# Twelve-sublayer decoder: in two mixture-of-experts sublayers, the late chunks' reciprocal standard deviation moves from GpSimd's power to VectorE and ScalarE's root

## The reference, cut to what matters

```python
def _layernorm(x, axis=-1, eps=1e-05):
    m = jnp.mean(x, axis=axis, keepdims=True)
    v = jnp.var(x, axis=axis, keepdims=True)
    return (x - m) / jnp.sqrt(v + eps)
...
x = _layernorm(x + _L1_ffn_ref(x, ...), axis=-1)     # sublayer 6
...
x = _layernorm(x + _L3_ffn_ref(x, ...), axis=-1)     # sublayer 12, the last
```

```python
def _L1_ffn_ref(x, router_w, router_b, weights1, bias1, weights2, bias2):   # 32 experts, hidden 32
    logits = x_flat @ router_w.T + router_b
    routed_idx = jnp.argmax(logits, axis=-1)
    h = jax.nn.relu(x_flat @ w1 + b1); y = jax.nn.relu(h @ w2 + b2)         # for each expert
    out_flat = y_all[routed_idx, jnp.arange(n)]

def _L3_ffn_ref(x, wg, W1, b1, W2, b2):                                     # 8 experts, hidden 512
    scores = jax.nn.softmax(xf @ wg, axis=-1); top1 = jnp.argmax(scores, axis=-1)
    h = jax.nn.gelu(jnp.einsum('ecd,edf->ecf', eb, W1) + b1[:, None, :], approximate=False)
    y = jnp.einsum('ecf,efd->ecd', h, W2) + b2[:, None, :]
    out_flat = jnp.where(valid[:, None], gathered, 0.0) * combine_w[:, None]
```

## Time and profile before

| | us |
|---|---|
| median of 3 runs | 3607.47 |
| lowest and highest of them | 3604.95, 3610.28 |
| profiled execution, its own time | 3619.05 |
| span of its trace | 3616.9 |
| granted TensorE clock, mean | 0.885 of full speed |
| sublayer 6: first late gather to the last copy's end | 1823.14 to 1881.59 |
| last sublayer: last tile's eviction to the last normalisation's end | 3564.43 to 3607.76 |

### The profile page before, as it was taken

How to read it: one execution, slowest core, us unless ns; L and a number is a source line. 1 busy time by engine, 2 the same in 40 slices (tenths; PEclk the granted TensorE clock), 3 DMA queues, 4 the chain that set the end, 5 groups by cost and what they waited for, 6 DMA issues and landing times. The chain is left out here.

```text
span 3616.9 us, 83245 instructions
## 1 busy us (share of the span) xinstructions
PE 2818.4 (78%) x28638; PEld 1992.1 (55%) x28638; DVE 2157.7 (60%) x5986; ACT 1818.0 (50%) x3448; POOL 1838.9 (51%) x1774
## 2 busy tenths in 40 slices
PE   2259985698999799953529998997888779992993
PEld 2258974475666466632416665654444446662893
DVE  2101324655888688862337886777999778872124
ACT  0024543553666566611216665775567776660451
POOL 3721245544888755525465555664133755555226
PEclk9679998898999899975559999998999899995997
DMA  8246763120111111114611112221000012212584
GB/s 296 86 135 217 233 199 90 39 8 14 43 47 46 55 51 70 67 40 136 164 53 43 56 54 68 89 87 44 1 1 1 8 30 73 76 54 88 178 249 128
DMA packets 321561, 308.86 MB, mean 85 GB/s; under 512 B 110950, under 2 KB 244489, under 8 KB 320908
## 3 DMA queue, kind: packets, MB, share of 16 engines
q1 hardware_dynamic: 279644, 255.42, 22.9%
q0 software_dynamic: 16384, 33.59, 3.1%
q10 hardware_dynamic: 25264, 16.40, 1.5%
HBM read 167.28 MB, written 60.69 MB: 63 GB/s over the span
## 5 line engine op out<-in xcount | busy, mean ns | idle before, releaser
L956 DVE TENSOR_TENSOR moe_first_tile_y<-moe_first_out_ps,moe_first_expert_w 128x256 f32<-128x256 f32 x85 | 35.7, 423 | 377.7 <-PE moe_first_out_ps L1092 248.1
L1092 PE MATMUL moe_first_out_ps<-moe_first_expert_w,moe_first_hid 128*128 128x128 f32 x1360 | 181.7, 280 | 75.0 <-issue 73.5
L1092 PEld LDWEIGHTS moe_first_out_ps<-moe_first_expert_w,moe_first_hid 128*128 128x128 f32 x1360 | 174.2, 196 | 85.8 <-issue 80.2
L814 POOL DMA_INDIRECT moe_first_token_y<-slot_y,moe_first_slots x128 | 124.6, 974 | 175.0 <-DMA slot_y<-moe_first_tile_y 137.0
L1913 POOL TENSOR_TENSOR causal_k_blocks<-causal_k_T,headmask 128x1024 f32<-128x1024 f32 x64 | 121.5, 1899 | 96.5 <-PE causal_scores L1518 94.5
L1165 POOL DMA_INDIRECT slot_x<-x_tok,moe_first_slots x128 | 123.5, 965 | 87.7 <-DVE moe_first_slots L928 49.3
L1913 POOL TENSOR_TENSOR alibi_k_blocks<-alibi_k_T,headmask 128x1024 f32<-128x1024 f32 x64 | 121.3, 1898 | 91.3 <-PE alibi_scores L1518 90.0
L1913 POOL TENSOR_TENSOR full_k_blocks<-full_k_T,headmask 128x1024 f32<-128x1024 f32 x64 | 120.8, 1898 | 82.2 <-PE full_scores L1518 80.0
L3211 PE MATMUL L_ffn_experts<-weights_odd,x_T 128*128 128x512 f32 x256 | 138.1, 622 | 11.6 <-ACT L_ffn_expert_out L3311 11.5
L1913 POOL TENSOR_TENSOR keys_k_blocks<-keys_k_T,headmask 128x1024 f32<-128x1024 f32 x64 | 120.9, 1900 | 46.7 <-PE keys_scores L1518 45.6
L3134 DVE SCALAR_TENSOR_TENSOR L_ffn_combined<-L_ffn_expert_out,L_ffn_mix,L_ffn_combined 128x128 f32<-128x128 f32 x448 | 139.0, 373 | 3.9
(11 more groups left out here) (634 smaller groups left out, 9005.9 us busy)
## 6 DMA issues: line engine op xcount, KB each, us to landing
moe_first_expert_w<-in_L_attn_experts SPq DMA_DIRECT2D x85, 578.0 KB
moe_last_expert_w<-in_L_ffn_experts SPq DMA_DIRECT2D x53, 578.0 KB
moe_first_tile_x<-slot_x SPq DMA_DIRECT2D x85, 128.0 KB
slot_y<-moe_first_tile_y SPq DMA_DIRECT2D x85, 128.0 KB
slot_x<-blank ACTq DMA_DIRECT2D x2, 4992.0 KB
L_ffn_tile_x<-slot_x SPq DMA_DIRECT2D x32, 256.0 KB
slot_y<-L_ffn_tile_y SPq DMA_DIRECT2D x32, 256.0 KB
moe_last_tile_x<-slot_x SPq DMA_DIRECT2D x53, 128.0 KB
```

The lines of the kernel that those rows point to most:

```text
L814: pool.indirect_dma_start(y_in[:, p, k, r, :], None, slot_y[part][0:NTS[part] * SLOT_TILE, :], bass.IndirectOffsetOnAxis(slots[:, part, r, ...
L956: dve.tensor_tensor(y_out[:, q, :, :], out_bank[j % 2][:, 0:SLOT_TILE].rearrange("p (s d) -> p s d", s=SPAN), over(wall[:, j % RING, 2 * F ...
L1092: last = pe.matmul(out_bank[j % 2][:, D * s:D * s + D], hid[:, j % 3, b, TILE * s:TILE * s + TILE], wall[:, j % RING, FF + D * b:FF + D * ...
```

## The change

For the late chunks of the two sublayers, `inverse_std` on GpSimd is dropped. `own_std` on VectorE adds epsilon, waits for ScalarE's root (`std_act`) and takes the reciprocal; VectorE then normalises the same chunk at once, ahead of the next chunk's sum. GpSimd's late loop holds gathers alone. ScalarE in sublayer 6 runs the root of chunk c + 1 ahead of the copy of chunk c. Early chunks, and `moe_first`, stay as they were.

```diff
@@ class RowTail
+        if n_early is not None:
+            self.n_early, self.std, self.std_done = n_early, sb("ln_std", [128, 2, PER]), sem("ln_std_done")
...
+    def own_std(self, dve, c):
+        p = c % 2
+        dve.wait_ge(self.moments_done, c + 1)
+        dve.tensor_scalar(self.ve[:, p, :], self.mv[:, p, :, 1], LN_EPS, None, ALU.add).then_inc(self.ve_done, 1)
+        dve.wait_ge(self.std_done, c + 1 - self.n_early)
+        dve.reciprocal(self.rstd[:, p, :], self.std[:, p, :]).then_inc(self.rstd_done, 1)
+
+    def std_act(self, act, c):
+        p = c % 2
+        act.wait_ge(self.ve_done, c + 1)
+        act.activation(self.std[:, p, :], self.ve[:, p, :], ACT.Sqrt).then_inc(self.std_done, 1)
@@ moe, VectorE
                 for c in late:
                     combine(dve, c)
-                    if c != late[0]:
-                        tail.normalise(dve, c - 1)
-                if late:
-                    tail.normalise(dve, late[-1])
+                    tail.own_std(dve, c)
+                    tail.normalise(dve, c)
@@ moe, ScalarE
                 for c in late:
+                    tail.std_act(act, c)
                     tail.copy_transposed(act, c, route_bank)
@@ moe, GpSimd
-                for c in late:
-                    if c + 1 < CHUNKS:
-                        gather(pool, c + 1, range(PER))
-                    tail.inverse_std(pool, c)
+                for c in late[:-1]:
+                    gather(pool, c + 1, range(PER))
@@ moe_small, ScalarE
+                tail.std_act(act, late[0])
                 for c in late:
+                    if c != late[-1]:
+                        tail.std_act(act, c + 1)
                     tail.copy_transposed(act, c, xT_bank)
@@ moe_small, GpSimd
                     if (c + 1) % PC:
                         gather(c + 1)
-                    tail.inverse_std(pool, c)
+                    if c not in late:
+                        tail.inverse_std(pool, c)
```

More of the change, by code:

```diff
@@ L573, with __init__ @@
 class RowTail:
-    def __init__(self, sub, final, on_act=False):
+    def __init__(self, sub, final, on_act=False, n_early=None):
         self.net, self.final, self.on_act = sub.net, final, on_act
@@ L724, in moe @@
         y_in = sub.sb("token_y", [128, 2, PER, top, D])
-        tail = RowTail(sub, final)
+        tail = RowTail(sub, final, n_early=None if hand_over else 0)
         sub.ctx = ctx
@@ L784, in moe @@
         held = range(FIRST, CHUNKS)
+        if not hand_over:
+            tail.n_early = FIRST
         after_tile = {due(c): c for c in range(FIRST)}
@@ L2673, in moe_small @@
         y_in = sb("token_y", [128, 2, PER, D])
-        tail = RowTail(sub, final)
+        tail = RowTail(sub, final, n_early=PC)
         out_banks = ctx.enter_context(nc.psum_tensor(f"{name}_out_ps", [128, 4, 512], F32))
```

## The result

| | before | after |
|---|---|---|
| median, us | 3606.21 (4 runs, 3602.99 to 3610.28) | 3582.34 (4 runs, 3579.23 to 3584.26) |
| ratio | | 0.9936, 95% interval 0.9922 to 0.9949 |
| span of the profiled execution | 3616.9 | 3577.2 |
| sublayer 6, first late gather to the next sublayer's first operation | 1823.14 to 1887.19, 64.05 | 1805.20 to 1858.50, 53.30 |
| last sublayer, chunk 10's first gather to the end | 3563.53 to 3616.9, 53.4 | 3533.88 to 3577.2, 43.3 |

The change saves 23.9 in the medians, 18 to 28 by the interval. A second timing of the same kernel, in a later series on a chip on which the kernel before had a median of 3619.07, gave 3600.10, a ratio of 0.9952 (0.9936 to 0.9967), 19.0 less.

What follows compares the result with a forecast made beforehand. GpSimd's issue of gathers was taken to set the pace in both stretches. Layer 1's 9.3 and the last sublayer's 8.0 gave 17.2 (rounded terms) off the median 3607.47: 3590.3, bounds 3588.3 to 3595, with scatter 3585.5 to 3598.

Steps and rivals of the forecast that it cites:

- gathers of sublayer 6: Layer 1's late gathers on GpSimd, without powers between them, end 8.2 us earlier (6.6 to 9.7).
- root's way: Both ends, chunk 15's moments to normalisation: 1.48 becomes 0.70 via VectorE and ScalarE, 0.78 less each.
- gathers of the last sublayer: Last sublayer's late gathers on GpSimd, without powers between them, end 7.2 us earlier (5.9 to 7.4).
- End of layer 1: TensorE's last transposes: chunk 14's earlier copy frees the bank before the last normalisation ends, some 0.3 more saved.
- hits: Gathers starting just behind VectorE's sum take 1.47, costing 0.52 each; none to six in layer 1, three taken, 1.56.
- Hidden, with 0.7 us to spare: VectorE waiting out the root: last-sublayer chunk takes 4.3 against 5.02 of the gathers, so no cost.
- the 26 scatters: Last sublayer's row scatter, 26 seen in one go, later ones still 0.96 + 0.30: no sign of long goes slowing.
- signs of being wrong: Profile after: gathers over 1.4 apart, landings above 2.5, VectorE idling for ScalarE above 1.2, or a differing stretch between.
- VectorE's work starves the gathers: Rival, both stretches: gathers of 1.60 beside VectorE, pace 1.90, 9.4 slower, 3617; chance 0.03.
- The loads lie open: Rival, ScalarE's three new activation-table loads uncovered, costing 3.8: 13.4 saved, 3594; chance 0.04.
- Only one stretch gains: Rival: the last sublayer's 7.2 goes (3597.5) or layer 1's 8.2 goes (3598.5); chance 0.08.
- nothing changes: Rival: transfers, not issue, set the pace, so faster issue only lengthens the landing; 3607, chance 0.05.

Runs made afterwards that it cites:

- The wait that computes nothing: Changed kernel with GpSimd held at its program's end, in both stretches, until the reciprocal of chunk 15; ratio 0.9970 to the kernel before.
- spacers: Changed kernel with a GpSimd memset of 512 elements a partition behind every four late gathers; ratio 0.9939 to the kernel before.
- the first experiment: Kernel before with only chunk 15's root moved off GpSimd in both stretches, powers between gathers kept; ratio 0.9986.

## Why the prediction was right in its direction and wrong in its size

| term | forecast | first trace |
|---|---|---|
| gathers of sublayer 6 | 8.2 | 5.75 |
| the end of sublayer 6 (root's way and last copy) | 1.1 | 5.0 |
| gathers of the last sublayer | 7.2 | 4.1 |
| its end (root's way) | 0.8 | 5.9 |
| sum | 17.2 | 20.8 |

**The step that failed first: the ends.** "The root's way" and "End of layer 1" priced the last power by the chain of VectorE, TensorE and ScalarE behind it. That chain did as forecast: reciprocal 0.44 behind the addition, normalisation 0.68 behind the moments (0.70 forecast); from the last gather to the last copy's end 8.23 before and 7.20 after, 1.03 less (1.1 forecast). But it was not the path. Before, GpSimd's drain was through 4.7 later than that chain, and it follows GpSimd's last operation, so the whole time from the last gather to the end of the last power was to be won: 5.0 and 5.9. One row of the kernel before would have said so, the next sublayer's memset with 8.83 of idling ended by GpSimd's own queue; the prediction had read the ends only as far as the last copy and the last normalisation. The wait that computes nothing (8.9 in the traces), and the last root put back (12.5), show it by themselves. After the change the two ways are within 0.7 of each other (1857.6 against 1856.9).

**The second: the pace of the gathers in a long go.** 1.25 apart is right, and none of the three forecast "hits" of 0.52 came: 31 of the 32 late gathers of sublayer 6 took 1.03 or less (the second trace has one hit, 1.46). Without the pause the gathers would have ended 44.47 - 4.57 = 39.9 behind the first, 10.3 earlier than before. "Hidden, with 0.7 us to spare" for VectorE failed: its work is as forecast (3.7 a chunk where it runs freely), but its completions came late, once by 4.5. The bound of the range for this term had only the hits in it. The prediction had looked for a slow gather in long goes (the 26 scatters), not for what happens to the engine beside it. Two of its signs of being wrong did show: a sum 3.18 behind its gathers (2.5 was the sign), and VectorE idling 1.38 for ScalarE in the last sublayer, at 3557.96 (1.2 was the sign).

The two errors have opposite signs, 10.9 - 1.9 = 9.0 too little at the ends and 15.4 - 9.9 = 5.5 too much in the gathers. The net is 3.6 more than forecast. That the sum of 17.2 comes so near to the 20.8 is therefore luck: by its own account of the ends (1.9) and the gathers as they ran (9.9) it would have been 11.8. It is the ends that carried the time past the lower end of the range. The rest of the 6.7 in the medians is not explained by the traces; the second timing lacks it.

**The rivals.** *VectorE's work starves the gathers* did not come as told: no gather at 1.60 in either stretch, and a gather in the middle of a normalisation took 0.95:

```profile
1819.63 1.12 DVE L659 TENSOR_SCALAR x_tok<-L_ffn_resid_sum,L_ffn_ln_moments,L_ffn_ln_rstd 128x128 f32<-128x128 f32 x4
1820.43 0.95 POOL L2985 DMA_INDIRECT L_ffn_token_y<-slot_y,L_ffn_slots  x1 [0.30 <-issue]
```

The longest gather behind the first was 1.02, at 1815.36, also beside a normalisation. The Trainium skill (SBUF — State Buffer, Who interferes with whom) has GpSimd locked out for the whole of a tensor_scalar in a two-port mode; no such hold-up is in these rows, and no row shows whether the instruction ran in that mode. The two engines did hurt each other, in the other direction: beside gathers at this pace VectorE's steps start late. *The loads lie open*: not in the changed kernel. They stand at 1805.99 and 3528.58, long before the first root, and at 1865.62 in the next attention, 1.28 each. The price is real, as the first experiment shows, where one lay open: 1.31 from the copy's end (1869.29) to the root's start (1870.60). *Only one stretch gains* and *nothing changes*: both stretches gained, 10.75 and 10.1.

**What stays open.** Why VectorE's steps start late. Shown is that it comes with gathers at 5.0 to 5.2 for four and not at 5.4, that starts more than 1 late begin 11 to 20 gathers into such a go, and that they move with the go and not with the program. Extra records and semaphore updates of ScalarE did not bring it on beside spacers. Not shown is what the gathers hold up. The trace of such a go is also short of releasers ("issue" and "remote" where a semaphore was waited for), and every time here is of an execution with records taken; whether an execution without them has the stall was not tried.

## What to carry to other kernels

Ask of every stage what lets the next one begin, and read the first row of the next stage in the profile before costing the last rows of this one: an operation last on the engine whose drain is longest costs its whole lateness, even if nobody waits for its result. Behind indirect transfers GpSimd's drain was long here, so let GpSimd finish first, or drain it once where it idles for longer than the drain takes. And when a wait is taken out of a steady alternation, the alternation may have kept a neighbour in time: look for a long unbroken go in the trace before relying on the pace of a short one, and try a small spacer.

## What the runs showed of the hardware that was not expected

GpSimd's drain at the end of a block, counted from its last operation, took 2.5 with 24 indirect transfers since the last drain, 2.9 with 32, 4.0 with 48, 5.3 with 64, 6.6 with 80, and 7.9 to 9.2 with 96 to 128. It didn't grow further: with over 200, in the sublayer moe_first, it took 7.3. In the attentions, where GpSimd only computes, it took about 0.1. That it is the number of transfers, and not something that goes along with it, is argued from the runs with added drains, where only the place of the drain was changed.

VectorE's steps that wait for VectorE's own completion started 1.1 to 4.5 late in unbroken goes of gathers 1.25 to 1.28 apart, in all six traces that had such goes of 20 or more, and not in the four with a gap of 0.7 behind every four. In goes of 12 and 16 they came up to 2.1 late in three stretches of six.
